# A graph network on one core: ScalarE's side work is dealt out between the pieces of a gather's step, and the softmax mixing of a Chebyshev layer gets an operand in PSUM and three places of mixed rows

## The chip, the cores and the metric

The kernel runs on one core of a Trainium2 chip. The metric is the time of one execution on the device, in microseconds, as the median of several runs. The engines are TensorE (PE, with its weight loads as PEld), VectorE (DVE), ScalarE (ACT), GpSimd (POOL) and SyncE (SP); each works through its own list of instructions in order, and they wait for one another through semaphores.

## The reference, cut to what matters

100,000 nodes with 96 features each, 50,000 edges, everything in f32. Four layers, each followed by a residual sum and a layer norm:

```python
x = layernorm(x + propagate_10_hops(x))
x = layernorm(x + prelu(segment_sum(norm * (x @ W)[row], col) + b))            # GCN
feats = [cheb(x, prop, w2, b2), cheb(x, prop, w3, b3), cheb(x, prop, w4, b4)]  # 2, 3 and 4 terms
scale = softmax(concat(feats) @ attn_w + attn_b)                               # three weights for a node
h = concat([feats[i] * scale[:, i:i + 1] for i in range(3)]) @ fus_w + fus_b
x = layernorm(x + relu(batchnorm(h)))
for W0, b0, W1, b1 in two_layers:                                              # GINE
    h = relu(relu((h + segment_sum(relu(h[src] + e), dst)) @ W0 + b0) @ W1 + b1)
x = layernorm(x + h)
```

A node without any edge gets nothing from its neighbours, so its rows need only products ("dense" work on its own row). Those rows are worked beside the passes that gather for the edges.

## The kernel before

The edges are sorted by destination and laid out as 128 lines of 392. An edge pass (`edge_pass`) walks over them in 56 steps of 7 edges a line. In a step POOL issues seven indirect DMAs (L527, 128 rows of 96 each, five steps ahead, into a ring of eight places); ACT multiplies the seven rows by their weights (L648; in the GINE passes DVE adds the edge features first and ACT takes the relu of four and of three rows at once, L644), in two parts of 4 and 3 that are signalled apart; DVE runs a chain of eight dependent instructions (L593) that sums the rows of one destination along a line, the first four needing the first part; ACT copies the sums out of PSUM (L1894 one by one with a factor, L1897 by parts); SP stores them.

Beside the gathers run jobs, whose work is cut into units q of four 128-row groups, two units to a batch i of eight groups. `share` spreads the units of a job evenly over the 56 steps. A job has a method for each engine, called once for each unit of the step, behind the step's own work on that engine.

- The dense Chebyshev job (`ChebRows`, tiles `cheb_base_*`, 98 units and a few to drain it, in the first and the second Chebyshev pass, here cheb1 at 9090 to 9696 us and cheb2 right behind): PE turns four groups around and multiplies each by a 97x292 matrix into one of four PSUM banks (`product`); ACT copies the turned rows (L1466) and the four products (L1590, "mixing" for short) into one of two places of mixed rows; DVE takes the three scores' maximum and differences (`scores`, L1510 to L1516), ACT the exponential (L1595), and DVE mixes the three features by the softmax (`mix`, L1553 to L1559); PE sums the mixed rows and their squares (L1639). A unit of even number computes scores, a unit of odd number mixes, so a two-unit step runs both, and in which order depends on the number that it starts with: 25 of the 56 steps of a pass start odd, 25 start even, 6 have one unit.
- The GINE and GCN jobs (`GineRows`, `GcnRows`): turn, copy (L1135), first product, relu by ACT (L1238), second product into one of two PSUM banks, and DVE takes it (L1216). The first GINE pass (12060 to 12596 us) has 31 steps of four units and 25 of three; the second (13075 to 13620 us) and the GCN pass (8090 to 8670 us) have 48 steps of two units and 8 of one.

What a two-unit step asks of ACT stands in this order: the seven sums of the step before, the seven weighings, then for each unit the copy, the mixings or the relu, and the exponential. DVE runs the chain and then the units, PE the units alone.

## Time and profile before

| | us |
|---|---|
| runs | 14193.84 median, 14192.54 to 14209.78 |
| the profiled execution, and its span | 14198.33, 14196.6 |
| busy DVE, POOL, PE, ACT | 7825.3 (55%), 8106.4 (57%), 5531.4 (39%), 4278.8 (30%) |
| gathers L527: GCN, both dense Chebyshev passes and the narrow one, GINE 1, GINE 2 (busy) | 382.8, 443.9 and 816.6, 378.1, 395.5 |
| PE at L1631 in the dense Chebyshev job | 562.3, idle in front of it 176.4 |

The span is a row of passes, each begun when the one before is done, so the shares over the whole say little; each pass has its own limit. A row of windows begins with the stretch and its length, and has the instructions of each engine in brackets. In a group by line the first number behind the bar is its busy time, the second the mean of one in ns, then the idle time of the engine in front of it and what ended that. The granted clock of PE differs from stage to stage (1.00 is 2.4 GHz, 0.50 is 1.2 GHz).

### The profile page before, as it was taken

The page shows a single profiled execution, that of the slowest core. Times are in us where ns is not written, and L with a number is a line of the kernel's source. Part 1 is how long each engine was busy: PE and PEld are TensorE (multiplying, and loading weights), DVE is VectorE, ACT ScalarE, POOL GpSimd, SP SyncE. Part 2 cuts the span into 40 slices and gives each one's busy share as a digit, 9 for nine tenths or more (in the row PEclk, how much of TensorE's full clock was granted, in tenths as well). Part 3 has the DMA queues.
Part 4 walks back from the last instruction along what each step waited for, and adds up shares of the span by engine and source line. Part 5 has one row for each costly group of instructions (what it writes and reads, how often), then busy time and mean ns, then how long its engine had stood idle before and what let it go on. Part 6 is the DMA issues. An engine that isn't in the chain of part 4 may idle for free. (4 is left out here: it accounts for less than half of the span.)

```text
span 14196.6 us, 114341 instructions
## 1 busy us (share of the span) xinstructions
PE 5531.4 (39%) x29175; PEld 4412.4 (31%) x29175; DVE 7825.3 (55%) x13637; ACT 4278.8 (30%) x11012; POOL 8106.4 (57%) x8280
## 2 busy tenths in 40 slices
PE   0000002000000000200004787776767987888876
PEld 0000002000000000200003565555546987666544
DVE  8880245444444444532274256576755755567865
ACT  0000011100000000100065565466644269554421
POOL 0557777777777777777704771277773000731767
PEclk9955555555555555555556768887778988899555
DMA  7300134434334433421176554444466678776743
GB/s 223 115 5 1 43 83 138 120 114 119 114 113 116 116 114 115 138 77 54 50 243 188 154 152 140 127 142 126 137 222 223 229 257 292 256 248 232 231 162 110
DMA packets 955755, 2071.60 MB, mean 146 GB/s; under 512 B 318457, under 2 KB 323855, under 8 KB 938976
## 3 DMA queue, kind: packets, MB, share of 16 engines
q1 hardware_dynamic: 689376, 1702.87, 35.0%
q0 software_dynamic: 265728, 361.43, 11.4%
q8 instruction: 241, 3.95, 0.1%
q14 instruction: 410, 3.36, 0.1%
HBM read 1251.36 MB, written 822.13 MB: 146 GB/s over the span
## 5 line engine op out<-in xcount | busy, mean ns | idle before, releaser
L731 POOL DMA_INDIRECT hop_raw<-hop_table,i_hop x2352 | 2219.5, 944 | 734.5 <-issue 686.3
L825 PE MATMUL hop_rows<-hop_chain,src_carries 128*128 128x96 f32 x12 | 4.3, 451 | 3023.7 <-DVE hop_chain L801 3023.7
L527 POOL DMA_INDIRECT gine_raw<-x,i_near x392 | 378.1, 965 | 1368.3 <-POOLq L89 1249.2
L755 DVE TENSOR_TENSOR hop_rows<-hop_raw,hop_factors 128x672 f32<-128x672 f32 x336 | 289.9, 863 | 1494.2 <-DMA hop_raw<-hop_table,i_hop 1494.2
L833 ACT ACTIVATE hop_keeps<-src_inner 128x672 f32<-128x672 f32 x336 | 255.4, 762 | 2665.1 <-DVE hop_chain L801 2613.0
L527 POOL DMA_INDIRECT cheb_raw<-cheb_table,i_cheb x784 | 816.6, 1042 | 245.1 <-issue 235.9
L825 PEld LDWEIGHTS hop_rows<-hop_chain,src_carries 128*128 128x128 f32 x12 | 3.0, 312 | 3025.0 <-issue 3025.0
L527 POOL DMA_INDIRECT cheb_raw<-x,i_near x392 | 443.9, 1132 | 546.0 <-POOLq L89 426.8
L527 POOL DMA_INDIRECT gine_raw<-conv,i_near x392 | 395.5, 1009 | 604.7 <-POOLq L89 485.5
L1794 POOL DMA_INDIRECT own_raw<-x,i_dst x392 | 370.0, 944 | 592.9 <-POOLq L89 473.7
L1631 PE MATMUL cheb_base_product<-folded,cheb_base_turned_rows 97*128 97x292 f32 x1568 | 562.3, 515 | 176.4 <-ACT cheb_base_mixed L1590 176.4
L801 DVE TENSOR_TENSOR_SCAN hop_chain<-hop_keeps,hop_rows 128x672 f32<-128x672 f32 x336 | 522.0, 1554 | 11.6
L996 POOL DMA_INDIRECT out_dram<-gine_slots_ends_rows,dst_end x392 | 424.3, 1083 | 151.8 <-issue 105.4
L299 POOL DMA_INDIRECT x_and_map<-sort_dst_entry,src_map_end x392 | 392.7, 1002 | 130.2 <-issue 129.2
L527 POOL DMA_INDIRECT gcn_raw<-x,dst_other x392 | 382.8, 977 | 127.6 <-issue 116.2
L299 POOL DMA_INDIRECT x_and_map<-map_dst_entry,dst_map_end x392 | 380.9, 972 | 127.9 <-issue 127.0
L1631 PE MATMUL cheb_slots_ends_product<-folded,b_slots_ends_turned_rows 96*128 96x292 f32 (+2 forms) x2352 | 452.9, 336 | 0.9 <-DVE cheb_slots_ends_part L1494 0.8
L2010 POOL DMA_INDIRECT hop_sums<-hop_last_sums,src_end x392 | 383.7, 979 | 119.4 <-issue 119.4
L1631 PEld LDWEIGHTS cheb_base_product<-folded,cheb_base_turned_rows 97*128 97x128 f32 x1568 | 354.4, 237 | 299.1 <-ACT cheb_base_mixed L1590 184.1
L731 POOL DMA_INDIRECT hop_first_raw<-x_and_map,src_other x392 | 369.9, 944 | 131.6 <-issue 119.2
L731 POOL DMA_INDIRECT hop_last_raw<-hop_table,i_hop x392 | 373.4, 953 | 122.5 <-issue 119.2
L731 POOL DMA_INDIRECT hop_second_raw<-hop_table,i_hop x392 | 369.9, 944 | 125.0 <-issue 114.6
(558 smaller groups left out, 22238.3 us busy)
## 6 DMA issues: line engine op xcount, KB each, us to landing
hop_res<-hop_table SPq DMA_DIRECT2D x336, 336.0 KB
hop_table<-hop_sums SPq DMA_DIRECT2D x336, 336.0 KB, 2.3
part<-cheb_put_mixed SPq DMA_DIRECT2D x49, 1168.0 KB, 6.8
cheb_slots_ends_part<-part SPq DMA_DIRECT2D x49, 1168.0 KB
start_x_x<-x_and_map SPq DMA_DIRECT2D x98, 400.0 KB, 3.7
x<-start_x_rows SPq DMA_DIRECT2D x98, 400.0 KB, 2.7
cheb_base_term<-x SPq DMA_DIRECT2D x98, 400.0 KB, 3.7
mid<-cheb_base_rows SPq DMA_DIRECT2D x98, 400.0 KB
```

Of the source, the lines that this page charges most:

```text
L299: pool.indirect_dma_start(out=self.node_map, out_offset=bass.IndirectOffsetOnAxis(ap=side.map_end[:, t:t + 1], axis=0), in_=self.entry[:, ...
L527: pool.indirect_dma_start(out=raw_rows[:, b % RAW, g, :], out_offset=None, in_=table, in_offset=bass.IndirectOffsetOnAxis(ap=index[:, t:t ...
L731: pool.indirect_dma_start(out=raw_rows[:, b % RAW, g, :], out_offset=None, in_=table, in_offset=bass.IndirectOffsetOnAxis(ap=index[:, t:t ...
L755: nc.vector.tensor_tensor(by_channel(b).rearrange("p c t -> p t c"), raw[:, b % RAW, :, :], spread(weights[:, at], C), ALU.mult).then_inc( ...
L801: nc.vector.tensor_tensor_scan(line(chain), line(keeps), rows[b % LINES], 0.0, ALU.mult, ALU.add)\
L825: nc.tensor.matmul(carried, side.carries[:, :], chain[:, (batches - 1) % LINES, :, EDGE - 1], start=True, stop=True).then_inc(s["carried"], 1)
L833: nc.scalar.activation(keeps[:, b % LINES, :, :], side.inner[:, b * EDGE:(b + 1) * EDGE].unsqueeze(1).to_broadcast([P, C, EDGE]), ACT.Copy ...
L996: pool.indirect_dma_start(out=table, out_offset=bass.IndirectOffsetOnAxis(ap=side.end[:, t:t + 1], axis=0), in_=self.wide_rows[:, m, g, :] ...
L1631: ins = nc.tensor.matmul(into[:, start:], self.turned_rows[0:rows, q % 2, j, c, :], self.k.folded[0:rows, power, start:MIX], start=(j == 0 ...
L1794: pool.indirect_dma_start(out=raw[:, b % RAW, g, :], out_offset=None, in_=table, in_offset=bass.IndirectOffsetOnAxis(ap=index[:, t:t + 1], ...
L2010: pool.indirect_dma_start(out=self.out, out_offset=bass.IndirectOffsetOnAxis(ap=ph.edge["side"].end[:, t:t + 1], axis=0), in_=ph.edge["sum ...
```

## The change

On ACT the method `scalar` of a job falls into pieces (`scalar_early`) and a rest (`scalar_late`). A unit of dense Chebyshev has four pieces: the copy and the first mixing, and the three other mixings one by one; a GINE or GCN unit has two, the copy and the relu. The pieces of a step's units are dealt in equal shares to four places: behind the first part of the sums, behind the second, behind the first part of the weighings, behind the second. The exponential, and the squares and roots of the norms, stay at the end of the step. In the dense Chebyshev job, three things change with it: the scores and the products of two features with their weights move from SBUF into one PSUM bank (`weigh`); for that bank, `product` has three places in place of four; and the mixed rows have three places in place of two. The products in PSUM have room for four groups of one feature, so DVE works by halves.

```diff
             for b in range(batches):
                 h, w = b % RAW, b % WORK
-                if jobs and b:
-                    finish.scalar(ph, act, b - 1)
+                for q in range(len(PARTS)):
+                    if jobs and b:
+                        finish.scalar_part(ph, act, b - 1, q)
+                    early(b, q)
...
                     ins.then_inc(s["weighed"], 1)
+                    early(b, len(PARTS) + q)
...
                 for job in jobs:
                     for q in share(job, b, batches):
-                        job.scalar(ph, act, q)
+                        job.scalar_late(ph, act, q)
...
+            def early(b, part):
+                for job in jobs:
+                    steps = share(job, b, batches)
+                    count = len(steps) * job.PIECES
+                    for u in range(part * count // (2 * len(PARTS)), (part + 1) * count // (2 * len(PARTS))):
+                        job.scalar_early(ph, act, steps[u // job.PIECES], u % job.PIECES)
...
-    SLOTS = 2
+    SLOTS = 3
...
+        self.PIECES = 0 if part_out else 1 if self.narrow else 4
...
+                weigh = ph.psum(f"{self.tag}_weigh", [P, 512])
+                self.weighted = weigh[:, 0:4 * C].rearrange("p (g c) -> p g c", c=C)
+                self.score = weigh[:, 4 * C:4 * C + 6 * self.GROUP].rearrange("p (n g s) -> p n g s", n=2, s=3)
...
-        self.product = [ph.psum(f"{self.tag}_product{n}", [P, 512]) for n in range(4)]
+        self.places = 4 if self.part_out or self.narrow else 3
+        self.product = [ph.psum(f"{self.tag}_product{n}", [P, 512]) for n in range(self.places)]
...
+            whole = slice(0, self.GROUP)
+            weighed(rows, whole, 0)
+            if self.dense:
+                for g in (slice(0, 4), slice(4, 8)):
+                    for n in (1, 2):
+                        weighed(self.weighted, g, n)
+                        own.wait()
+                        own.step(nc.vector.tensor_tensor(rows[:, g, :], rows[:, g, :], self.weighted, ALU.add))
+                        own.wait()
...
-            if q:
-                self.taken_one(ph, pe, q - 1, c)
-            into = self.product[c][:, 0:MIX]
+            self.place_free(ph, pe, q, c)
+            into = self.product[(4 * q + c) % self.places][:, 0:MIX]
```

`weighed(into, g, n)` is one `tensor_tensor` of feature n with its weight; `place_free` waits for the product three before to be taken. The instructions of PE, SP and POOL stand in the order in which they stood.

ACT in a two-unit step of the dense Chebyshev job, from the sums (L1894, now L1940) over the weighings (L648, now L657), the copies (L1466, now L1492) and the mixings (L1590, now L1628) to the exponential (L1595, now L1637), before:

```order
L1894 ACTIVATE cheb_sums<-cheb_total,f_cheb 128x96 x7
L648 ACTIVATE cheb_rows<-cheb_raw,w_cheb 128x96 x7
L1466 ACTIVATE cheb_base_turned_rows<-cheb_base_turned 96x512
L1590 ACTIVATE cheb_base_mixed<-cheb_base_product 128x292 x4
L1466 ACTIVATE cheb_base_turned_rows<-cheb_base_turned 96x512
L1590 ACTIVATE cheb_base_mixed<-cheb_base_product 128x292 x4
L1595 ACTIVATE cheb_base_score<-cheb_base_score 128x24
```

and now:

```order
L1940 ACTIVATE cheb_sums<-cheb_total,f_cheb 128x96 x4
L1492 ACTIVATE cheb_base_turned_rows<-cheb_base_turned 96x512
L1628 ACTIVATE cheb_base_mixed<-cheb_base_product 128x292 x2
L1940 ACTIVATE cheb_sums<-cheb_total,f_cheb 128x96 x3
L1628 ACTIVATE cheb_base_mixed<-cheb_base_product 128x292 x2
L657 ACTIVATE cheb_rows<-cheb_raw,w_cheb 128x96 x4
L1492 ACTIVATE cheb_base_turned_rows<-cheb_base_turned 96x512
L1628 ACTIVATE cheb_base_mixed<-cheb_base_product 128x292 x2
L657 ACTIVATE cheb_rows<-cheb_raw,w_cheb 128x96 x3
L1628 ACTIVATE cheb_base_mixed<-cheb_base_product 128x292 x2
L1637 ACTIVATE cheb_base_weigh<-cheb_base_weigh 128x24
```

A copy and four mixings now stand in front of the step's first weighing, and a copy and two mixings between its two parts.

ACT in a four-unit step of the first GINE pass (L1897, now L1943, the sums; L644, now L653, the weighings; L1135, now L1155, the copies; L1238, now L1258, the relus), before:

```order
L1897 ACTIVATE gine_sums<-gine_total 128x384
L1897 ACTIVATE gine_sums<-gine_total 128x288
L644 ACTIVATE gine_rows<-gine_raw 128x384
L644 ACTIVATE gine_rows<-gine_raw 128x288
L1135 ACTIVATE gine_conv_turned_rows<-gine_conv_turned 96x512
L1238 ACTIVATE gine_conv_hidden_rows<-gine_conv_hidden,gine_conv_c 96x512
L1135 ACTIVATE gine_conv_turned_rows<-gine_conv_turned 96x512
L1238 ACTIVATE gine_conv_hidden_rows<-gine_conv_hidden,gine_conv_c 96x512
```

(two more such pairs follow) and now:

```order
L1943 ACTIVATE gine_sums<-gine_total 128x384
L1155 ACTIVATE gine_conv_turned_rows<-gine_conv_turned 96x512
L1258 ACTIVATE gine_conv_hidden_rows<-gine_conv_hidden,gine_conv_c 96x512
L1943 ACTIVATE gine_sums<-gine_total 128x288
L1155 ACTIVATE gine_conv_turned_rows<-gine_conv_turned 96x512
L1258 ACTIVATE gine_conv_hidden_rows<-gine_conv_hidden,gine_conv_c 96x512
L653 ACTIVATE gine_rows<-gine_raw 128x384
L1155 ACTIVATE gine_conv_turned_rows<-gine_conv_turned 96x512
L1258 ACTIVATE gine_conv_hidden_rows<-gine_conv_hidden,gine_conv_c 96x512
L653 ACTIVATE gine_rows<-gine_raw 128x288
L1155 ACTIVATE gine_conv_turned_rows<-gine_conv_turned 96x512
L1258 ACTIVATE gine_conv_hidden_rows<-gine_conv_hidden,gine_conv_c 96x512
```

The second weighing, behind no unit before, is now behind three.

DVE at the dense softmax mixing, before:

```order
L1545 TENSOR_TENSOR cheb_base_score<-cheb_base_score,cheb_base_most 128x24
L1553 TENSOR_TENSOR cheb_base_rows<-cheb_base_mixed,cheb_base_score 128x8x96
L1554 TENSOR_TENSOR cheb_base_weighted<-cheb_base_mixed,cheb_base_score 128x768
L1555 TENSOR_TENSOR cheb_base_weighted<-cheb_base_mixed,cheb_base_score 128x768
L1557 TENSOR_TENSOR cheb_base_rows<-cheb_base_rows,cheb_base_weighted 128x8x96
L1559 TENSOR_TENSOR cheb_base_rows<-cheb_base_rows,cheb_base_weighted 128x8x96
```

and now:

```order
L1572 TENSOR_TENSOR cheb_base_weigh<-cheb_base_weigh,cheb_base_most 128x24
L1579 TENSOR_TENSOR cheb_base_rows<-cheb_base_mixed,cheb_base_weigh 128x8x96
L1579 TENSOR_TENSOR cheb_base_weigh<-cheb_base_mixed,cheb_base_weigh 128x384
L1588 TENSOR_TENSOR cheb_base_rows<-cheb_base_rows,cheb_base_weigh 128x4x96
L1579 TENSOR_TENSOR cheb_base_weigh<-cheb_base_mixed,cheb_base_weigh 128x384
L1588 TENSOR_TENSOR cheb_base_rows<-cheb_base_rows,cheb_base_weigh 128x4x96
L1579 TENSOR_TENSOR cheb_base_weigh<-cheb_base_mixed,cheb_base_weigh 128x384
L1588 TENSOR_TENSOR cheb_base_rows<-cheb_base_rows,cheb_base_weigh 128x4x96
L1579 TENSOR_TENSOR cheb_base_weigh<-cheb_base_mixed,cheb_base_weigh 128x384
L1588 TENSOR_TENSOR cheb_base_rows<-cheb_base_rows,cheb_base_weigh 128x4x96
```

Five instructions of 768 columns become one of 768 and eight of 384, and each of the eight has one operand in PSUM.

## Rows read from the trace of the kernel before

**Rows 1.** Windows of three stretches: busy PE, PEld, DVE, ACT, POOL; clock, DMA, GB/s.

```profile
9090.00:9696.00 606.00, 418.30 (x1978) 324.35 (x1978) 423.78 (x1046) 375.81 (x1326) 445.53 (x393) 0.78 0.45 132
13075.00:13620.00 545.00, 410.60 (x1374) 278.47 (x1374) 419.62 (x851) 240.21 (x520) 397.15 (x393) 0.55 0.68 214
12321.00:12355.00 34.00, 31.49 (x203) 23.77 (x202) 20.79 (x51) 24.43 (x49) 26.08 (x27) 1.00 0.80 250
```

**Rows 2.** Groups by line, 9150 to 9650 us (cheb1).

```profile
L527 POOL DMA_INDIRECT cheb_raw<-x,i_near x345 | 396.1, 1148 | 105.1 <-issue 105.1
L648 ACT ACTIVATE cheb_rows<-cheb_raw,w_cheb 128x96 f32<-128x96 f32 x322 | 92.5, 428 | 0.0
```

**Rows 3.** Groups by line, 10305 to 10785 us (the narrow pass cheb3).

```profile
L527 POOL DMA_INDIRECT cheb_raw<-cheb_table,i_cheb x385 | 363.5, 944 | 117.3 <-issue 114.9 <-ACT cheb_rows L648 2.4
```

**Rows 4.** Waits, 9150 to 9650 us: total us, count, median.

```profile
ACT cheb_base_mixed L1590 <- DVEq L1561: 119.5, 44, 5.7
DVE cheb_total L593 <- ACT cheb_rows L648: 82.0, 24, 3.5
```

**Rows 5.** Timeline, cheb1 step starting odd: start, busy us, instruction, [idle before].

```profile
9402.51 0.33 DVE L593 SCALAR_TENSOR_TENSOR cheb_total<-cheb_bridge,dst_joins,cheb_rows 128x96 f32<-128x96 f32 x1 [3.51 <-ACT cheb_rows L648]
...
9409.93 0.96 DVE L1559 TENSOR_TENSOR cheb_base_rows<-cheb_base_rows,cheb_base_weighted 128x768 f32<-128x768 f32 x1
9410.98 1.33 ACT L1590 ACTIVATE cheb_base_mixed<-cheb_base_product 128x292 f32<-128x292 f32 x4 [5.59 <-DVEq L1561]
9411.42 0.18 DVE L1516 TENSOR_TENSOR cheb_base_score<-cheb_base_mixed,cheb_base_most 128x24 f32<-128x24 f32 x1
9411.45 4.26 PE L1631 MATMUL cheb_base_product<-folded,cheb_base_turned_rows 97*128 97x292 f32 x8 [4.47 <-ACT cheb_base_mixed L1590]
9412.17 0.24 ACT L1595 ACTIVATE cheb_base_score<-cheb_base_score 128x24 f32<-128x24 f32 x1
9412.28 1.75 ACT L1894 ACTIVATE cheb_sums<-cheb_total,f_cheb 128x96 f32<-128x96 f32 x7
9413.84 2.02 ACT L648 ACTIVATE cheb_rows<-cheb_raw,w_cheb 128x96 f32<-128x96 f32 x7
9415.11 0.33 DVE L593 SCALAR_TENSOR_TENSOR cheb_total<-cheb_bridge,dst_joins,cheb_rows 128x96 f32<-128x96 f32 x1 [3.51 <-ACT cheb_rows L648]
9415.50 1.88 PE L1639 MATMUL cheb_base_sum<-cheb_base_rows 128*96 128x97 f32 x16
9415.70 0.61 ACT L1466 ACTIVATE cheb_base_turned_rows<-cheb_base_turned 96x512 f32<-96x512 f32 x1
9416.17 1.34 ACT L1590 ACTIVATE cheb_base_mixed<-cheb_base_product 128x292 f32<-128x292 f32 x4
```

**Rows 6.** Timeline of a cheb1 step that starts even.

```profile
9433.18 0.33 DVE L593 SCALAR_TENSOR_TENSOR cheb_total<-cheb_bridge,dst_joins,cheb_rows 128x96 f32<-128x96 f32 x1 [0.24 <-DVE cheb_base_rows L1559]
```

**Rows 7.** Groups by line over the whole span.

```profile
L1494 DVE TENSOR_TENSOR cheb_slots_ends_part<-cheb_slots_ends_part,cheb_slots_ends_product 128x292 f32<-128x292 f32 x392 | 167.1, 456 | 164.2 <-PE cheb_slots_ends_product L1631 153.9 <-DVE cheb_slots_ends_rows L1559 10.1
L774 DVE TENSOR_TENSOR hop_rows<-hop_chain,hop_factors 128x672 f32<-128x672 f32 x336 | 289.4, 861 | 11.6
L527 POOL DMA_INDIRECT gine_raw<-x,i_near x392 | 378.1, 965 | 1368.3 <-POOLq L89 1249.2 <-issue 118.6 <-ACT gine_rows L644 0.6
```

**Rows 8.** Timeline of a step of the first GINE pass.

```profile
12292.33 0.85 ACT L644 ACTIVATE gine_rows<-gine_raw 128x384 f32<-128x384 f32 x2
12293.92 0.60 PE L1157 MATMUL gine_conv_turned<-ident,gine_conv_x 128*96 128x128 f32 x4
12295.22 1.03 PE L1165 MATMUL gine_conv_product<-gine_conv_w,gine_conv_hidden_rows 97*128 97x96 f32 x8
12295.42 0.68 ACT L1238 ACTIVATE gine_conv_hidden_rows<-gine_conv_hidden,gine_conv_c 96x512 f32<-96x512 f32 x1 [0.27 <-PE gine_conv_hidden L1253]
```

**Rows 9.** Timeline of a step of the second GINE pass.

```profile
13322.21 0.33 DVE L593 SCALAR_TENSOR_TENSOR gine_total<-gine_bridge,dst_joins,gine_rows 128x96 f32<-128x96 f32 x1 [0.69 <-ACT gine_rows L644]
```

More of the change, by code:

```diff
@@ L1093, in scalar_setup, with scalar_early, scalar_late, scalar @@
     def scalar_setup(self, ph, act): pass
-    def scalar(self, ph, act, q): pass
+    def scalar_early(self, ph, act, q, n): pass
+    def scalar_late(self, ph, act, q):
+        self.scalar_norm(ph, act, q)
+    def scalar(self, ph, act, q):
+        for n in range(self.PIECES):
+            self.scalar_early(ph, act, q, n)
+        self.scalar_late(ph, act, q)
     def tensor_setup(self, ph, pe): pass
@@ L1493, in vector @@
                 dve.wait_ge(self.sem(ph, "product"), 4 * q + c + 1)
-                self.nc.vector.tensor_tensor(into, into, self.product[c][:, 0:MIX], ALU.add)\
+                self.nc.vector.tensor_tensor(into, into, self.product[(4 * q + c) % self.places][:, 0:MIX], ALU.add)\
                     .then_inc(self.sem(ph, "taken"), 1)
@@ L1524, in taken_all, with place_free @@
             eng.wait_ge(self.sem(ph, "taken"), 8 * i + 8)
-    def taken_one(self, ph, eng, q, c):
-        if self.part_out:
-            eng.wait_ge(self.sem(ph, "moved" if c % 2 else "taken"), 2 * q + c // 2 + 1)
-        else:
-            eng.wait_ge(self.sem(ph, "taken"), 4 * q + c + 1)
+    def place_free(self, ph, eng, q, c):
+        before = 4 * q + c - self.places
+        if before >= 0 and self.part_out:
+            eng.wait_ge(self.sem(ph, "moved" if c % 2 else "taken"), before // 2 + 1)
+        elif before >= 0:
+            eng.wait_ge(self.sem(ph, "taken"), before + 1)
     def mix(self, ph, dve, i):
@@ L1549, in mix, with weighed @@
             own.wait()
-            def weighted(n):
-                return self.mixed[:, m, :, n * C:(n + 1) * C], spread(score[:, :, n], C)
-            own.step(nc.vector.tensor_tensor(rows, *weighted(0), ALU.mult))
-            own.step(nc.vector.tensor_tensor(self.part[:, 0, :, :], *weighted(1), ALU.mult))
-            own.step(nc.vector.tensor_tensor(self.part[:, 1, :, :], *weighted(2), ALU.mult))
-            own.wait()
-            own.step(nc.vector.tensor_tensor(rows, rows, self.part[:, 0, :, :], ALU.add))
-            own.wait()
-            own.step(nc.vector.tensor_tensor(rows, rows, self.part[:, 1, :, :], ALU.add))
-            own.wait()
+            def weighed(into, g, n):
+                own.step(nc.vector.tensor_tensor(into, self.mixed[:, m, g, n * C:(n + 1) * C], spread(score[:, g, n], C),
+                                                 ALU.mult))
+            whole = slice(0, self.GROUP)
+            weighed(rows, whole, 0)
+            if self.dense:
+                for g in (slice(0, 4), slice(4, 8)):
[4 more added lines that the diff above has]
+                        own.wait()
+            else:
+                for n in (1, 2):
+                    weighed(self.weighted[:, n - 1, :, :], whole, n)
+                own.wait()
+                for n in (1, 2):
+                    own.step(nc.vector.tensor_tensor(rows, rows, self.weighted[:, n - 1, :, :], ALU.add))
+                    own.wait()
             dve.sem_inc(self.sem(ph, "ready"), 1)
@@ L1587, in scalar, with scalar_late @@
                     act.wait_ge(self.sem(ph, "ready"), i - slots + 1)
-            for c in ((0, 2) if self.part_out else range(4)):
+            for c in ((0, 2) if self.part_out else range(4) if self.PIECES == 1 else (n,)):
                 act.wait_ge(self.sem(ph, "product"), 4 * q + c + 1)
-                nc.scalar.activation(self.mixed[:, m, q % 2 * 4 + c, :], self.product[c][:, 0:MIX], ACT.Copy)\
+                what = self.product[(4 * q + c) % self.places][:, 0:MIX]
+                nc.scalar.activation(self.mixed[:, m, q % 2 * 4 + c, :], what, ACT.Copy)\
                   .then_inc(self.sem(ph, "taken"), 1)
+    def scalar_late(self, ph, act, q):
         i = q // 2 - 1
+        if self.part_out and self.PIECES == 0:
+            self.scalar_early(ph, act, q, 0)
         if not self.part_out and q % 2 == 0 and 0 <= i < self.count:
             act.wait_ge(self.sem(ph, "scored"), i + 1)
-            nc.scalar.activation(self.score[:, i % 2, :, :], self.score[:, i % 2, :, :], ACT.Exp)\
+            self.nc.scalar.activation(self.score[:, i % 2, :, :], self.score[:, i % 2, :, :], ACT.Exp)\
               .then_inc(self.sem(ph, "exponent"), 1)
@@ L1886, in scalar, with scalar_part @@
     def scalar(self, ph, act, b):
+        for q in range(len(PARTS)):
+            self.scalar_part(ph, act, b, q)
+    def scalar_part(self, ph, act, b, q):
         e, s = ph.edge, ph.sems
-        self.slot_free(ph, act, b)
-        for q, (g0, n) in enumerate(PARTS):
-            bank = e["total"][b % e["sets"] * len(PARTS) + q]
-            act.wait_ge(s["chained"], b * STEPS + g0 + n + 1)
-            if e["scale"] is not None:
-                for g in range(g0, g0 + n):
-                    ins = self.nc.scalar.activation(e["sums"][:, b % WORK, g, :], bank[:, g - g0, :], ACT.Copy,
-                                                    scale=e["scale"][:, b * EDGE + g:b * EDGE + g + 1])
-            else:
-                ins = self.nc.scalar.activation(e["sums"][:, b % WORK, g0:g0 + n, :], bank[:, 0:n, :], ACT.Copy)
-            ins.then_inc(s["copied"], 1)
+        g0, n = PARTS[q]
+        if q == 0:
+            self.slot_free(ph, act, b)
+        bank = e["total"][b % e["sets"] * len(PARTS) + q]
+        act.wait_ge(s["chained"], b * STEPS + g0 + n + 1)
+        if e["scale"] is not None:
+            for g in range(g0, g0 + n):
+                ins = self.nc.scalar.activation(e["sums"][:, b % WORK, g, :], bank[:, g - g0, :], ACT.Copy,
+                                                scale=e["scale"][:, b * EDGE + g:b * EDGE + g + 1])
+        else:
+            ins = self.nc.scalar.activation(e["sums"][:, b % WORK, g0:g0 + n, :], bank[:, 0:n, :], ACT.Copy)
+        ins.then_inc(s["copied"], 1)
 class Residual:
```

34 lines of the change are left out of this document (18 added, 16 removed).

## The prediction

> **What bounds the kernel now.** The kernel is a row of passes, so I looked for the bound of each pass with a dense job. I began with the windows by stage: in the first dense Chebyshev pass (cheb1) the reader sees no engine over 74% busy (POOL 445.5 of 606 us, DVE 423.8, PE 418.3, ACT 375.8, granted clock 0.78), so either POOL's issue sets the pace, or a loop of waits through several engines [rows 1]. The groups by line decide: POOL's gathers take 1148 ns and wait for nothing but their issue (105.1 us over 345 of them), and the weighing L648 was never idle in front [rows 2]. So gathered rows always lie ready when ACT comes for them, and ACT, not POOL, is behind. POOL by its own pace would need (396.1 + 105.1) / 345 × 392 = 569 us of the 606. The waits show the loop: the chain L593 waits 82.0 us for weighings, and ACT's mixings wait 119.5 us for DVE to finish with a place of mixed rows [rows 4].
>
> The timeline shows where. A step that starts with an odd unit lasts from chain to chain 9415.11 − 9402.51 = 12.60 us [rows 5]. DVE ends its softmax mixing at 9410.89, and from there 4.22 us pass to the next chain, all on ACT: four mixings that waited for that place (9410.98 to 9412.17, 1.19 us), the exponential .11, seven sums 1.56, the weighings up to the chain's start 1.27 [rows 5]. In a step that starts even, the chain follows DVE's own last addition with .24 us: DVE is the bound there [rows 6]. With 25 steps of each sort a pass, the odd ones pay for every microsecond that ACT puts between DVE's mixing and the next weighing.
>
> **The change part by part.** *Odd steps of the dense Chebyshev passes (50 in the two passes).* The exponential stays at the step's end and still waits for scores that DVE takes behind its mixing. The third place of mixed rows takes the wait of 5.59 us away from the mixings [rows 5]; but what is late next is the exponential, at the same point of DVE's work. From DVE's mixing to the next chain stand now: the scores, .71 (9410.89 to 9411.60) and .05 to the wake-up; the exponential .11; seven sums 1.56; a copy .47 (9415.70 to 9416.17); four mixings 1.19; four weighings 1.27. That is 5.36 in place of 4.22: +1.14 [rows 5]. The chain's first four instructions (some 1.4 us) cover the second weighing only if it comes within that time; in front of it stand a copy .47, two mixings .60, and its own three rows .80, 1.87 in all: +.4. DVE's mixing gets longer as worked out below: +.9. That makes +2.4 where PE keeps up.
>
> PE must keep up with three places. At the copy of the step PE is at most three products ahead. The fourth needs the place that the first mixing frees; behind it in PE's row stand a sum and the turn of the next unit, whose copy ACT wants before the second weighing, and two more products. At half clock that is 1.07 (a quarter of 4.26) + 1.88 + .60 + 2.13 + a mixing .30 = 6.0 us behind the first mixing, where ACT by itself would be there after 3.9 (.30 + .67 + .60 + 1.27 + .47 + .60): +2.1 [rows 5, 8]. And PE, for which two units with a sum take 2 × 4.26 + 1.88 + 2 × .60 = 11.6 us at half clock, comes about 2 us late to the next odd step after the work that it could not do ahead; so +6.6 to +6.8, I take 6.8. At full clock these times halve, and a slip of about .6 is left: +3.0. The pass ran at .78, more than half of it at full clock [rows 1], and the step shown is one at half clock: 11.6 us for its 40 instructions are .29 each, where the pass has 418.3 / 1978 = .21 [rows 1, 5]. A longer pass leaves PE busy a smaller share, which did not keep the clock up in GINE 2 (.55 [rows 1]); I take a value near the middle, +4.8. 50 × 4.8 = +240 (ends: 50 × 2.4 = +120 and 50 × 6.8 = +340).
>
> *DVE's mixing.* An instruction of 128x768 with two SBUF operands took .958 us (.96 in the timeline), one of 128x292 with an operand in PSUM 456 ns [rows 5, 7]. The line through both, 148 ns + 1.055 ns a column, gives 553 ns for 384. Eight of these and one of .958 are 5.38, five of .958 were 4.79: +.6. Six more waits of DVE for itself at about .035 (L774 was idle 11.6 us over 336 such waits [rows 7]), and an overlap of about .1 lost where instructions followed without a wait: +.9. In the 50 even steps this stands on DVE's own path: 50 × .94 = +47 (ends +30 and +60).
>
> The Trainium skill ("VectorE: DVE Perf Modes", The TRN2 errata) gives a vector instruction with a PSUM source 62 cycles more than one from SBUF; by an estimate from that page, .065 us × 9 × 98 mixings, the sum would be about 57 us higher. The line through the two rows above shows nothing of that.
>
> *First GINE pass.* PE needs 31.49 us for 203 instructions at full clock, 14 a unit: 2.17 us a unit; in GINE 2 at about half clock 410.6 / 98 = 4.19 [rows 1]. DVE takes the product of a step's first unit only behind the chain, whose second half needs the second weighing, which now stands behind three of four units (four of six pieces in a three-unit step). PE has two product banks, so the third product waits for all of this. Between PE's last step before it and the product: a relu .68, the second weighing .43 (half of .85), four chain instructions 1.32, DVE's taking .55 (384 columns by the line above), wake-ups .2: 3.2 us of PE idle in a four-unit step [rows 7, 8]. In a three-unit step PE has some 1.8 us of other work meanwhile at full clock, so 1.4, and at half clock none. Steps of 4 × 2.17 + 3.2 = 11.9 (31 of them) and 3 × 2.17 + 1.4 = 7.9 (25) make 566 us, where POOL's gathers now set 378.1 + 118.6 = 497 [rows 7]: +69. At half clock 31 × 20.0 + 25 × 12.6 = 935: +438. A PE that idles a quarter of the step may lose its clock; I saw both levels under such jobs (1.00 and .55 [rows 1]) and take half of the time at each: 705, so +208.
>
> *Second GINE pass and GCN.* In two-unit steps a copy .47 and a relu .68 come before the first weighing, for which the chain waits already now (.69) [rows 5, 8, 9]: at most 1.15 × 48 = +55, at least 0 where the gather or the edge features are late anyway; taken +35. GCN has the same steps, but there PE gets its copies earlier and DVE waits for PE's products; the two pull against each other: 0, within ± 25. Jobs that run beside no edge pass take their pieces in the order of before: 0.
>
> Sum against the profiled execution: 14,198 + 240 + 47 + 208 + 35 + 0 = 14,728. It stands 4 us over the median of the runs, so I say 14,725 us, +3.7%. With all low ends it is 14,198 + 120 + 30 + 69 + 0 − 25 = 14,390; with all high ends 14,198 + 340 + 60 + 438 + 55 + 25 = 15,115.
>
> **The rivals.** *POOL is freed and was the bound (faster).* The gathers took 1148 ns in cheb1 and 944 ns in the narrow pass, where the softmax mixing does not run beside them in this form [rows 2, 3]. If DVE's additions with both operands in SBUF hold up POOL's issue, and the loop above is only its shadow, then both dense passes fall to the pace of the narrow one: (363.5 + 117.3) / 385 × 392 = 490 us in place of POOL's own 569, 2 × 75 = −150, to 14,048. The point from which it decides is that a pair of an odd and an even step, now 22 us, gets through in 2 × 8.7. For it speaks the difference of 204 ns; against it that the weighing is never idle for lack of rows [rows 2], so that a faster gather finds ACT still behind. The Trainium skill says the same of the ports ("SBUF — State Buffer", Who interferes with whom: a vector instruction with two SBUF inputs contends with a GpSimd instruction that reads SBUF). The two means agree with it. I expect the shorter gathers, and no time from them. Chance .10, with .02 more for a smaller gain from the earlier pieces alone.
>
> *Only Chebyshev pays.* If DVE's taking in the GINE passes finds slack (PE stays at full clock and POOL's five steps ahead even the long and the short steps out), their terms fall to nothing: 14,198 + 240 + 47 = 14,485. For it: the GINE gathers waited .6 us for ACT in the whole pass [rows 7]. Against it: PE was 93% busy in the fast window [rows 1], so idle time of 3.2 us a step cannot be made up. Chance .15.
>
> *GINE 1 falls to half clock for good.* Then its term is +438: 14,728 + 230 = 14,958. For it: GINE 2 with a less busy PE ran at .55 [rows 1]. Against it: four units a step keep PE far busier. Chance .12.
>
> *No change to speak of*, gains and losses cancelling: .03.
>
> **How the numbers follow.** The forecast has .58, the rivals .12, .15, .12 and .03. The range leaves out the fast rival and the far end: 14,330 to 15,060. Slower by more than 0.2% (28 us, about what a measurement of this kernel can tell from no change) has .58 + .15 + .12 = .85, within it .03, faster .12.
>
> **What would show it.** Right: odd steps of cheb1 near 17 us from chain to chain, even ones near 10.4; the mixing of DVE near 5.4 us busy with 553 ns for 384 columns; gathers near 950 ns, and POOL's idle time put down to the weighing, where now it waits for nothing; in the first GINE pass PE idle in front of the second product for DVE's taking, some 3 us a step, and the pass well over 550 us. Wrong: the exponential not waiting for DVE in odd steps (then ACT's path is shorter than I have it); gathers that still pace cheb1 at 944 ns with a pass under 500 us; a first GINE pass that still follows its gathers.

## The result, and the profile after

The changed kernel takes 14,668.75 us (14,656.93 to 14,674.14) where the kernel before takes 14,198.44 beside it: 1.0327 times as long, 95% interval 1.0314 to 1.034. The forecast was 14,725. The profiled execution spans 14,655.2 us, 458.6 more than before. From the start of a pass's first gather to the start of the next pass's, read from POOL's rows of every kernel's trace, the passes stand so:

| kernel | median us | GCN and the stage behind it | cheb1 | cheb2 | GINE 1 and the stage behind it | GINE 2 | odd, even step |
|---|---|---|---|---|---|---|---|
| before | 14,198 | 1002.1 | 602.3 | 601.1 | 1011.4 | 570.5 | 12.6, 9.5 |
| changed | 14,669 | 977.9 | 725.9 | 723.9 | 1236.0 | 587.6 | 17.1, 10.2 |
| mixing_alone | 14,262 | 1002.2 | 633.8 | 630.9 | 1007.4 | 567.5 | 13.1, 10.2 |
| dealt_alone | 14,492 | 977.0 | 635.9 | 633.5 | 1243.4 | 587.6 | 14.0, 9.5 |
| three_places | 14,619 | 977.6 | 703.8 | 702.9 | 1223.7 | 585.3 | 17.1, 9.5 |
| both_weighed | 14,502 | 972.0 | 678.9 | 678.0 | 1172.5 | 590.0 | 15.0, 10.2 |
| exp_later | 14,506 | 979.1 | 646.7 | 645.5 | 1232.5 | 585.8 | 13.7, 10.2 |
| taken_first | 14,442 | 979.6 | 726.2 | 723.9 | 1007.5 | 588.1 | 17.1, 10.2 |
| later_psum | 14,160 | 977.0 | 593.6 | 590.8 | 1007.5 | 570.3 | 11.0, 10.2 |
| later_sbuf | 14,133 | 979.2 | 572.7 | 580.0 | 1008.9 | 567.0 | 10.0, 9.8 or 10.7 |
| later_sbuf_again | 14,136 | 980.0 | 576.3 | 583.6 | 1008.4 | 570.7 | 10.0, 10.7 |
| later_scores | 14,123 | 983.7 | 566.6 | 566.6 | 1019.5 | 567.3 | 11.0, 9.3 |

(The last column has the commonest length of a two-unit Chebyshev step, from one chain to the next.) One execution of later_psum (14,513 us) and one of later_sbuf (16,486 us) ran at a lower granted clock than the others of their kernel (.60 and .55 against .66); they stand in these medians, but not in the ratios given below. The changed kernel's +459 are +246 in the two dense Chebyshev passes, +225 in the first GINE pass, +17 in the second and −24 in GCN; all else moved by −5 in sum.

Windows of the changed kernel over cheb1 and the first GINE pass, in the columns of [rows 1]:

```profile
9065.00:9790.00 725.00, 425.57 (x1978) 327.31 (x1977) 458.14 (x1242) 382.02 (x1326) 369.89 (x392) 0.72 0.38 110
12278.00:12985.00 707.00, 563.79 (x2583) 404.27 (x2584) 269.35 (x654) 308.38 (x582) 376.39 (x392) 0.75 0.58 183
```

POOL is busy 370 us in cheb1 instead of 446, DVE 458 instead of 424, and the pass is 119 us longer: neither of the two engines sets its end. The groups by line of cheb1 (9130 to 9750 us), which answer to [rows 2], say why:

```profile
L527 POOL DMA_INDIRECT cheb_raw<-x,i_near x345 | 325.5, 943 | 262.5 <-ACT cheb_rows L657 162.8 <-issue 99.7
...
L1579 DVE TENSOR_TENSOR cheb_base_weigh<-cheb_base_mixed,cheb_base_weigh 128x384 f32<-128x384 f32 x180 | 100.8, 560 | 4.7
L1588 DVE TENSOR_TENSOR cheb_base_rows<-cheb_base_rows,cheb_base_weigh 128x384 f32<-128x384 f32 x180 | 99.6, 554 | 6.2
L657 ACT ACTIVATE cheb_rows<-cheb_raw,w_cheb 128x96 f32<-128x96 f32 x329 | 98.1, 385 | 0.0
...
L1579 DVE TENSOR_TENSOR cheb_base_rows<-cheb_base_mixed,cheb_base_weigh 128x768 f32<-128x768 f32 x45 | 42.9, 954 | 6.0 <-DVE cheb_base_weigh L1572 0.5
```

A gather takes 943 ns now instead of 1148, and POOL, which waited for nobody, waits 162.8 us for ScalarE's weighing to free a place of its ring. A faster gather bought a longer wait. The waits of the same stretch, which answer to [rows 4] (in a row of waits the third number is the longest single wait, not the median, as the heading there has it; the stretch here is 620 us long, there 500):

```profile
ACT cheb_base_weigh L1637 <- DVE cheb_base_weigh L1542: 245.3, 44, 8.3
PE cheb_base_product L1672 <- ACT cheb_base_mixed L1628: 239.3, 47, 9.1
DVE cheb_total L593 <- ACT cheb_rows L657: 167.5, 49, 5.1
```

The wait for a place of mixed rows (119.5 us) is gone, and the exponential's wait for DVE's scores, 47.2 us in the 500 before, stands in its place with 245.3; the chain waits 167.5 us instead of 82. PE's product, too, now waits long, for a mixing to free one of its three places. One odd step in the timeline, for [rows 5]:

```profile
9356.92 0.17 ACT L1637 ACTIVATE cheb_base_weigh<-cheb_base_weigh 128x24 f32<-128x24 f32 x1 [7.91 <-DVE cheb_base_weigh L1542]
9357.00 1.03 ACT L1940 ACTIVATE cheb_sums<-cheb_total,f_cheb 128x96 f32<-128x96 f32 x4
...
9357.89 0.60 ACT L1492 ACTIVATE cheb_base_turned_rows<-cheb_base_turned 96x512 f32<-96x512 f32 x1
9358.37 0.73 ACT L1628 ACTIVATE cheb_base_mixed<-cheb_base_product 128x292 f32<-128x292 f32 x2
...
9358.85 1.34 PE L1672 MATMUL cheb_base_product<-folded,cheb_base_turned_rows 97*128 97x292 f32 x2 [8.78 <-ACT cheb_base_mixed L1628]
...
9359.98 2.79 PE L1680 MATMUL cheb_base_sum<-cheb_base_rows 128*96 128x97 f32 x16
...
9360.57 1.17 ACT L657 ACTIVATE cheb_rows<-cheb_raw,w_cheb 128x96 f32<-128x96 f32 x4
9361.77 0.33 DVE L593 SCALAR_TENSOR_TENSOR cheb_total<-cheb_bridge,dst_joins,cheb_rows 128x96 f32<-128x96 f32 x1 [4.89 <-ACT cheb_rows L657]
...
9362.57 0.69 PE L1653 MATMUL cheb_base_turned<-ident,cheb_base_term 128*96 128x128 f32 x4
...
9363.10 2.13 PE L1672 MATMUL cheb_base_product<-folded,cheb_base_turned_rows 97*128 97x292 f32 x8
9363.30 0.59 ACT L1492 ACTIVATE cheb_base_turned_rows<-cheb_base_turned 96x512 f32<-96x512 f32 x1 [1.56 <-PE cheb_base_turned L1653]
...
9364.59 0.89 ACT L657 ACTIVATE cheb_rows<-cheb_raw,w_cheb 128x96 f32<-128x96 f32 x3
...
9365.52 1.05 DVE L593 SCALAR_TENSOR_TENSOR cheb_total<-cheb_total,dst_joins,cheb_rows 128x96 f32<-128x96 f32 x3 [2.33 <-ACT cheb_rows L657]
...
9372.68 0.55 DVE L1588 TENSOR_TENSOR cheb_base_rows<-cheb_base_rows,cheb_base_weigh 128x384 f32<-128x384 f32 x1
...
9378.81 0.33 DVE L593 SCALAR_TENSOR_TENSOR cheb_total<-cheb_bridge,dst_joins,cheb_rows 128x96 f32<-128x96 f32 x1 [4.84 <-ACT cheb_rows L657]
```

From the exponential at 9356.92 to the chain at 9361.77 ScalarE has sums, a copy, four mixings and four weighings in its path. The chain then stops in its middle for 2.33 us, since the second weighing stands behind a copy, and that copy behind PE: the fourth product (waiting 8.78 us for a place), the sum and the turn. The last two rows are the end of this step's mixing and the next chain, 17.04 us after the first.

Of the first GINE pass the waits (12300 to 12940 us) show who holds whom:

```profile
ACT gine_conv_turned_rows L1155 <- PE gine_conv_turned L1177: 259.2, 168, 5.0
DVE gine_total L593 <- ACT gine_rows L653: 223.2, 82, 6.5
...
POOL gine_raw L527 <- ACT gine_rows L653: 162.3, 34, 10.0
...
PE gine_conv_product L1185 <- DVE gine_conv_rows L1236: 98.1, 45, 3.2
```

Read together they look like a ring: DVE's chain waits for ScalarE, ScalarE's copies for PE, PE for DVE to take a product. Three experiments below test it. The gathers, which waited .6 us for ScalarE [rows 7], wait 162.3.

### The profile page after: what moved, and what is told of

It is laid out like the page before. It is cut to its first block and busy times, and to the rows that moved or that the text cites. A ratio compares the mean times of both kernels' runs of the same rounds, so it can differ in the third digit from the quotient of the medians.

```text
span 14655.2 us, 114731 instructions
## 1 busy us (share of the span) xinstructions
PE 5655.4 (39%) x29175; PEld 4475.7 (31%) x29175; DVE 7893.7 (54%) x14029; ACT 4302.6 (29%) x11012; POOL 7964.5 (54%) x8280
## 5 line engine op out<-in xcount | busy, mean ns | idle before, releaser
L527 POOL DMA_INDIRECT cheb_raw<-cheb_table,i_cheb x784 | 740.2, 944 | 400.1 <-issue 230.5
L527 POOL DMA_INDIRECT cheb_raw<-x,i_near x392 | 369.9, 944 | 698.1 <-POOLq L89 421.6
```

What stands on the lines that cost most here:

```text
L527: pool.indirect_dma_start(out=raw_rows[:, b % RAW, g, :], out_offset=None, in_=table, in_offset=bass.IndirectOffsetOnAxis(ap=index[:, t:t ...
```

## The experiments

**mixing_alone**: ScalarE's pieces back behind the weighings.

```diff
                 for job in jobs:
+                    if True:
+                        continue                                # in early
                     steps = share(job, b, batches)
...
-                        job.scalar_late(ph, act, q)
+                        (job.scalar if True else job.scalar_late)(ph, act, q)
```

> ScalarE's pieces are all put back behind the step's weighings, unit by unit; the mixing with its operand in PSUM, three product places and three places of mixed rows stay. My theory (the dealing costs, since the pieces stand between DVE's mixing and the next chain): GCN and both GINE passes fall back to their times of before (from start to start 1002, 1011 and 570 us), and the dense Chebyshev passes lose most of their 123 us each: in odd steps the path from DVE's mixing to the next chain is scores .76, exponential .1, sums 1.56, weighings 1.27 = 3.7 us instead of 4.22, the mixing .8 longer, so about 12.9 us (12.6 before, 17.1 changed), even steps 10.2 (9.5 before): about +30 us a pass, 14,260 in all. Rival 1 (three product places are the cost, PE late): odd steps stay at 15 us or more, 14,380 or more. Rival 2 (POOL was the bound and is freed now): the dense passes fall under 560 us each, 14,110 or less.

Measured 14,261.72 us, 1.0056 times before (1.0039 to 1.0073). The chain of two neighbouring odd steps:

```profile
9322.30 0.33 DVE L593 SCALAR_TENSOR_TENSOR cheb_total<-cheb_bridge,dst_joins,cheb_rows 128x96 f32<-128x96 f32 x1 [2.92 <-ACT cheb_rows L659]
9335.23 0.33 DVE L593 SCALAR_TENSOR_TENSOR cheb_total<-cheb_bridge,dst_joins,cheb_rows 128x96 f32<-128x96 f32 x1 [2.92 <-ACT cheb_rows L659]
```

12.93 us, where 12.9 was worked out; the commonest odd step is 13.1. The dense passes lose 31 and 30 us on before, the other passes are those of before, the first GINE pass among them: with no piece ahead of a weighing its 225 us are gone. The freed POOL won nothing:

```profile
L527 POOL DMA_INDIRECT cheb_raw<-x,i_near x319 | 301.1, 944 | 149.0 <-issue 92.2 <-ACT cheb_rows L659 56.9
```

Three product places cost little while no weighing stands behind a piece.

**dealt_alone** and **three_places**: the pieces dealt out, but the mixing in SBUF with its five instructions; then the same with three product places.

```diff
-            if self.dense:
+            if False:
                 weigh = ph.psum(f"{self.tag}_weigh", [P, 512])
...
-            if self.dense:
+            if False:
                 for g in (slice(0, 4), slice(4, 8)):
...
-        self.places = 4 if self.part_out or self.narrow else 3
+        self.places = 4      # dealt_alone only
```

> The pieces stay dealt out and the mixed rows keep three places, but scores and weighted features are in SBUF as before (five instructions of 768 columns) and the products have four places. My theory: GCN and GINE as in the changed kernel; in odd Chebyshev steps the fourth product is ready ahead, so PE's sum and turn begin some 1.1 us earlier and the second weighing with them, and the mixing is .8 shorter: 15 us (17.1 changed), even steps 9.5: about 655 us a pass (724), 14,530 in all; gathers back at about 1,140 ns without harm. Rival (the three places and the PSUM operand are most of the Chebyshev cost): odd steps near 13 us, passes near 610 us, 14,440.

> As dealt_alone (scores and weighted features in SBUF, pieces dealt out), but with three product places as in the changed kernel. Mixing alone cost 31 us a dense Chebyshev pass, dealing alone 34, both together 123. My theory (the fourth place is what joins them: with three, PE's fourth product, its sum and its turn wait for a mixing that now stands behind the first part of the sums): odd steps near 16.3 us (14.0 with four places; 17.1 less the .8 of the longer mixing), passes near 695 us, 14,610 in all. Rival (the longer mixing itself meets the dealt order): odd steps stay near 14 us, passes near 640, 14,500.

Measured 14,491.53 (1.0212, 1.0195 to 1.0229) and 14,619.42 us (1.0296, 1.0281 to 1.0311). In the Chebyshev passes mixing alone costs 31 us, dealing alone 34, dealing with three places 102. For dealt_alone I had expected odd steps of 15 us and passes of 655; with 14.0 and 636 it lies between that and the rival's 13 and 610. Where PE's sum stands in an odd step of dealt_alone:

```profile
9336.24 2.90 PE L1680 MATMUL cheb_base_sum<-cheb_base_rows 128*96 128x97 f32 x16 [5.36 <-DVEq L1597]
...
9336.88 0.22 ACT L1637 ACTIVATE cheb_base_score<-cheb_base_score 128x24 f32<-128x24 f32 x1 [7.00 <-DVE cheb_base_score L1542]
```

and in one of three_places:

```profile
9349.49 0.22 ACT L1637 ACTIVATE cheb_base_score<-cheb_base_score 128x24 f32<-128x24 f32 x1 [6.99 <-DVE cheb_base_score L1542]
...
9352.59 2.79 PE L1680 MATMUL cheb_base_sum<-cheb_base_rows 128*96 128x97 f32 x16
...
9355.18 1.06 PE L1653 MATMUL cheb_base_turned<-ident,cheb_base_term 128*96 128x128 f32 x4
...
9359.02 1.05 DVE L593 SCALAR_TENSOR_TENSOR cheb_total<-cheb_total,dst_joins,cheb_rows 128x96 f32<-128x96 f32 x3 [3.22 <-ACT cheb_rows L657]
```

With four places PE has all four products done and waits at its sum; the sum starts the moment DVE's mixing is over, .64 us ahead of the exponential. With three it stands behind a fourth product that waits for a dealt mixing, and starts 3.10 us behind the exponential, in the way of the turn that the second weighing needs. So my theory of the fourth place holds; the size I expected (16.3) does not: odd steps are 17.1 us with the short mixing as with the long one. In three_places the turn took 1.06 us against .69 in the changed kernel and the chain's halt was 3.2 to 3.3 against 2.33. Windows over single instructions of PE show its granted clock, third from the end as in [rows 1]: the turn and then the products in three_places, the same products and the sum in the changed kernel, and two sums of before:

```profile
9355.18:9356.24 1.06, 1.06 (x7) 1.03 (x6) 0.58 (x2) 0.00 (x0) 0.76 (x2) 0.50 0.20 48
9356.03:9358.57 2.54, 2.54 (x10) 1.85 (x9) 0.00 (x0) 1.79 (x5) 1.88 (x2) 0.77 0.20 40
...
9363.10:9365.07 1.97, 1.97 (x11) 1.46 (x10) 0.09 (x1) 1.75 (x5) 0.00 (x0) 1.00 0.00 0
9359.98:9362.57 2.59, 2.59 (x18) 2.59 (x16) 0.72 (x3) 1.61 (x6) 0.00 (x0) 0.50 0.43 168
...
9402.60:9404.12 1.52, 1.52 (x19) 1.51 (x18) 1.28 (x5) 1.52 (x6) 1.20 (x2) 1.00 0.75 266
9415.50:9417.38 1.88, 1.88 (x19) 1.88 (x18) 1.60 (x6) 1.88 (x8) 1.32 (x2) 0.80 0.98 352
```

In three_places the granted clock was .50 over the turn and .77 over the products behind it; in the changed kernel those products had 1.00. That accounts for the longer halt: .37 us on the turn, .57 on the eight products (2.70 against 2.13). The shorter mixing does save its .8 us, and PE, slower in just this stretch, loses them again. Why the clock rose later there was not tested.

**both_weighed**: the second weighing ahead of the third and fourth share.

```diff
                     ins.then_inc(s["weighed"], 1)
+                for q in range(len(PARTS)):
                     early(b, len(PARTS) + q)
```

> One piece of the order is changed: the two parts of the weighing stand together, and the third and fourth share of the pieces behind both. My prediction's step for the first GINE pass (PE's third product waits for the second weighing, which stands behind three units): the pass loses more than half of its 226 us. Rival (any unit ahead of the weighing ties the chain to PE's progress, since DVE takes a product only behind the chain and PE has two product places): worked out in the same way, the path from PE's last step to the taken product is then a relu .7, a weighing .45, the whole chain 2.9, the taking .55 and .2 = 4.8 us, of which PE fills 1.4 at full clock: 3.4 us idle instead of 3.2, so the pass stays within 40 us of 745. For odd Chebyshev steps both say: the second weighing no longer waits for PE's turn (2.3 us in the changed kernel), 14.8 us instead of 17.1, some 55 us a pass. In all 14,440 by the first, 14,560 by the rival.

Measured 14,501.87 us (1.0223, 1.0206 to 1.024). Chebyshev as both said (15.0 us, 46 us a pass). The first GINE pass won 64 of its 225 us: less than half, more than the rival's 40, so neither had the size. The chain still waits long for ScalarE in it (12200 to 12800 us):

```profile
DVE gine_total L593 <- ACT gine_rows L653: 169.9, 48, 6.5
```

**taken_first**: DVE takes the products of the first two units ahead of the chain.

```diff
+                for job in jobs:
+                    for q in share(job, b, batches)[:job.taken_first]:   # 2 in the first GINE pass
+                        job.vector(ph, dve, q)
                 for q, (g0, n) in enumerate(PARTS):
...
-                    for q in share(job, b, batches):
+                    for q in share(job, b, batches)[job.taken_first:]:
                         job.vector(ph, dve, q)
```

> As the changed kernel, but in the first GINE pass DVE takes the products of a step's first two units ahead of the chain instead of behind it. My theory (PE has two product places, and its third product waits until DVE has run the chain, whose weighings stand behind units that wait for PE): PE is no longer tied to the chain, and the pass falls from 745 us to about 600, 14,525 in all. Rival (ScalarE's copies and relus ahead of the weighings hold the chain up by themselves, since each waits for PE's turn of a later unit): within 40 us of 745, 14,660.

Measured 14,442.12 us (1.017, 1.0155 to 1.0184). The pass is back at its time of before and beyond what I expected: 1007.5 with the stage behind it, all of the 225 us. The window, and the gathers of 12310 to 12780 us:

```profile
12290.00:12800.00 510.00, 461.10 (x2672) 341.41 (x2673) 275.69 (x680) 317.83 (x611) 379.01 (x392) 0.90 0.80 262
```

```profile
L527 POOL DMA_INDIRECT gine_raw<-x,i_near x371 | 358.8, 967 | 113.1 <-issue 112.7 <-ACT gine_rows L656 0.3
```

ScalarE's order is the same as in the changed kernel, with the second weighing behind three units; PE's clock is .90 instead of .75, and the gathers set the pace again. So the ring is real, and it opens at either end: at DVE's taking, as here, or with no unit ahead of the weighings, as in mixing_alone. With two units still ahead of both weighings (both_weighed) it stays closed, only shorter.

**exp_later**: the exponential of a step's last unit, where even, behind the next step's second weighing.

```diff
                     ins.then_inc(s["weighed"], 1)
+                    if q:
+                        for job in jobs:
+                            for u in deferred(job, b - 1):     # the last unit, where it is even
+                                job.scalar_late(ph, act, u)
...
                     for q in share(job, b, batches):
-                        job.scalar_late(ph, act, q)
+                        if q not in deferred(job, b):
+                            job.scalar_late(ph, act, q)
```

> As the changed kernel, but where a step's last unit has an even number its exponential (the only thing in which ScalarE waits for DVE's mixing) is issued behind the next step's second weighing. DVE wants it only behind that step's chain. My theory (the exponential at the step's end ties sums, pieces and weighing to the end of DVE's mixing): odd steps fall from 17.1 us to what DVE (chain 2.9, mixing 6.5, scores .7) or PE at its clock (5.8 to 11.6) needs, 10.5 to 12: the dense passes near 590 us each, 14,400 in all. Rival (PE's order with three places is the tie): odd steps stay over 14 us, 14,550.

Measured 14,506.07 us (1.0225, 1.0207 to 1.0242): odd steps 13.7 us, under the rival's 14 and well over my 10.5 to 12. Waits of cheb1 (9130 to 9700 us):

```profile
PE cheb_base_sum L1692 <- DVEq L1609: 128.1, 45, 7.5
...
DVE cheb_total L593 <- ACT cheb_rows L661: 90.7, 23, 4.4
```

ScalarE runs ahead now and the chain hardly waits at its start (7.0 of the 90.7 us), but its second weighing waits through copy, turn and sum for DVE's mixing. Half of my theory held: the exponential was one tie, PE's sum is the next.

**later_psum, later_sbuf, later_scores**: pieces dealt out in GCN alone, the exponential moved as above; then the mixing in SBUF with four places; then the scores alone in PSUM, with three places.

```diff
+                    if not isinstance(job, GcnRows):
+                        continue                                # in early
...
+                        for n in range(0 if isinstance(job, GcnRows) else job.PIECES):
+                            job.scalar_early(ph, act, q, n)     # at the end of the step
...
+                self.score = weigh[:, 0:6 * self.GROUP].rearrange("p (n g s) -> p n g s", n=2, s=3)   # later_scores
```

> Dealt out in the GCN pass alone. In the other jobs the pieces stand behind the weighings, and in the dense Chebyshev steps whose last unit is even the exponential is issued behind the next step's weighings; mixing with its operand in PSUM, three product places, three places of mixed rows. In exp_later the odd steps stopped at 13.7 us since the second weighing stands behind a copy that waits for PE's sum, which waits for DVE's mixing; here no weighing stands behind a piece. My theory: odd steps near 11 us (12.6 before), even ones 10.2 (9.5), so 590 to 600 us a dense pass (602 before); GCN 24 us less than before, GINE as before: 14,150. Rival (PE at half clock, 11.6 us for a two-unit step with its sum, is next): odd steps 12.5, passes near 630, 14,215.

> As later_psum, with scores and weighted features in SBUF and four product places. My theory: DVE needs 9.5 us a step and would not wait for ScalarE, but POOL's gathers take 1,135 ns beside it, 7 x 1.44 = 10.1 us a step: this is where POOL's pace shows, 585 to 595 us a dense pass, 14,140 in all, and the operand in PSUM is worth nothing either way. Rival 1 (PE at half clock): as above, 620 or more, 14,200. Rival 2 (POOL's five steps ahead hide its pace in a pass of 56 steps): 560 us, 14,080.

> As later_sbuf, but the scores alone are in PSUM (a bank of their own, so three product places); the weighted features stay in SBUF, DVE's five instructions of 768 columns too. In later_sbuf ScalarE waited for gathers (95 us in 450), whose mean was 1,131 ns: POOL's pace of 10 us a step is the bound there. My theory (a gather's issue is held up by DVE instructions with both operands in SBUF; now the two additions are such, the three multiplications not): gathers at 944 + 2/5 x 187 = 1,020 ns, 9.3 us a step, under DVE's 9.5: dense passes near 560 us (573 and 580), 14,100 in all. Rival 1 (the additions alone hold the gathers up, or something else on DVE does): gathers stay near 1,120, passes as in later_sbuf, 14,130. Rival 2 (three places cost here too: PE late in odd steps, which were 11 us in later_psum against 10.2 of DVE): odd steps near 11, passes near 585, 14,150.

> The same kernel as later_sbuf, run beside later_scores on one chip: 14,120 to 14,145.

Measured 14,160.47 (0.9972, 0.9961 to 0.9983), 14,132.89 (0.9951, 0.9938 to 0.9964), 14,122.64 (0.9937, 0.9923 to 0.995) and, beside the last, later_sbuf again 14,136.17 (0.9945, 0.9931 to 0.9958): all below the kernel before, by .3 to .6%, and clear of their intervals. later_psum came out as expected (odd steps 11.0 us, even ones 10.2). Gathers and weighings in 9150 to 9600 us, of later_sbuf:

```profile
L527 POOL DMA_INDIRECT cheb_raw<-x,i_near x314 | 355.1, 1131 | 95.7 <-issue 89.0 <-ACT cheb_rows L663 6.7
...
L663 ACT ACTIVATE cheb_rows<-cheb_raw,w_cheb 128x96 f32<-128x96 f32 x315 | 88.5, 361 | 95.3 <-DMA cheb_raw<-x,i_near 95.3
```

of later_scores:

```profile
L527 POOL DMA_INDIRECT cheb_raw<-x,i_near x336 | 335.6, 999 | 102.4 <-issue 100.9 <-ACT cheb_rows L663 1.5
...
L663 ACT ACTIVATE cheb_rows<-cheb_raw,w_cheb 128x96 f32<-128x96 f32 x316 | 90.1, 413 | 0.0
```

and the gathers of later_psum:

```profile
L527 POOL DMA_INDIRECT cheb_raw<-x,i_near x330 | 311.5, 944 | 125.2 <-issue 94.5 <-ACT cheb_rows L663 30.8
```

In later_sbuf the weighing waits 95.3 us for gathers: with ScalarE's loop cut, POOL's pace is the bound, as the rival had it for a kernel that was not there yet. Its passes of 573 and 580 us are under the 585 to 595 that I had expected. With the scores in PSUM a gather takes 999 ns (1,020 expected) and that wait is gone; even steps fall to 9.3 us, while odd ones stay at 11 and over as rival 2 had it: PE's products wait 120.4 us for a place, where in later_sbuf they waited for nothing. The passes, 567 us each, lie between my 560 and that rival's 585, and are 10 and 17 us shorter than those of later_sbuf beside it, but its first GINE pass is 11 us longer, which is not explained; the two whole times are not told apart by their intervals.

## Why the prediction was right

**The bound.** Read rightly: gathers at 944 ns in mixing_alone and the changed kernel gave nothing, and the loop through ScalarE, DVE and PE decided. The faster rival needs that loop out of the way; only in later_sbuf, where it is, does POOL's pace show as the bound. (In that rival's sum 569 less 490 is 79 a pass, not 75; nothing hangs on it.)

**Odd steps.** Forecast +4.8, measured +4.5 (17.1), for two reasons that were both named: ScalarE's pieces between the exponential and the chain (4.85 us from 9356.92 to 9361.77, forecast 4.60) and the second weighing behind PE. The step shown above, 17.04 us, is longer than that of [rows 5] in three parts. From the mixing's end at 9373.23 to the next chain are 5.58 us, +1.36 (forecast +1.14). The chain's halt is 2.33 (forecast .4, and 2.1 more at half clock). The rest of the way from chain to mixing's end, .75, is the longer mixing (forecast +.9). What did not come is the fourth term at half clock, PE some 2 us late at the next odd step: it stood idle for 8.78 us in front of its fourth product. So the value "near the middle" hit in part by luck. The working for half clock read the step of [rows 5] as one at half clock, while it has both levels: its sum of 1.88 us ran at a mean of .80, where a sum took 2.79 at .50 and 1.52 at 1.00; and the turn's .60, from [rows 8] at 1.00, is 1.06 at .50.

**Even steps and the mixing.** Forecast +.94, measured 10.23 for 9.46: +.77. The instruction of 384 columns took 560 and 554 ns where the line through two rows gave 553. The Trainium skill's dearer PSUM source ("VectorE: DVE Perf Modes", The TRN2 errata; an estimate of 65 ns more each from that page) does not show. One line through a PSUM row and an SBUF row could not have shown it; what does is the same instruction of 768 columns, 958 ns with its scores in SBUF and 954 with them in PSUM. Both passes together: +287 forecast, +246 measured. A pass has 23 odd steps that mix, not the 25 of the sum, and the last of each row of them took 16.0 to 16.2 us: these steps make 100 of a pass's 123 us, the even ones 18.

**GINE 1.** Forecast +208, measured +225, and the step behind it was half wrong. Right was that PE, with two product places, waits for a taking that stands behind the chain: taken_first, which moves the takings alone, gave back all of it. Wrong was the weight I gave to the second weighing behind three units: moved up in both_weighed, it gave back only 64 us, since two units ahead of both weighings still make the chain wait for PE. The mean of two clock levels that I took (half of the time each, .75) is what the window has, and the steps lie between the two levels' sums: 15.9 us on the mean for four units (11.9 and 20.0), 9.7 for three (7.9 and 12.6). That the two levels would share the time so evenly was a guess.

**GINE 2 and GCN.** +35 forecast, +17 measured; 0 within 25 forecast, −24 measured. In GCN the earlier pieces let PE deliver before DVE asks. Waits of before, 8110 to 8590 us:

```profile
DVE gcn_total L593 <- ACT gcn_rows L648: 106.6, 48, 3.1
DVE gcn_base_rows L1342 <- PE gcn_base_product L1388: 66.4, 30, 4.2
```

and of the changed kernel:

```profile
DVE gcn_total L593 <- ACT gcn_rows L657: 149.1, 53, 3.9
...
DVE gcn_base_rows L1361 <- PE gcn_base_product L1407: 2.7, 4, 0.8
```

The chain waits 43 us more, the taking 64 us less: the two pull against each other as said, and the gain is the larger. In GINE 2 the chain's wait for weighings rose from 13.8 us (13095 to 13590 us) to 61.3 (13535 to 14030 us of the changed kernel), but its wait for gathers in front of the edge features fell from 54.3 to 35.4, the slack that I had allowed for. In sum the terms came out 71 us too high, 41 of it in the Chebyshev passes.

## What to carry to other kernels

An engine's instructions that are dealt out among the steps of a loop tie that loop to whatever each of them waits for: before moving one ahead of a signal, follow its wait to the end, and see whether it comes back to the signal. Look for the one instruction that waits for the end of another engine's step (here the exponential) and put it behind the work that the others are waiting for. A transfer made faster is worth nothing until the loop that consumes it is the shorter one; then it is worth trying again.

## What the runs showed that was not expected

A gather beside DVE's mixing took 1,131 ns on the mean with five instructions of two SBUF operands (later_sbuf), 999 with two of them left (later_scores) and 944 with none (later_psum). The two additions alone thus keep 55 of the 187 ns, less than two fifths. PE's sum of 16 instructions took 2.79 to 2.90 us in the odd steps shown, where PE had stood idle for 5 to 9 us ahead of it and the granted clock was .50; in the kernel before one took 1.52 at 1.00.
